# Four of 64 sets of expert weights loaded ahead of the experts stage instead of two, in one kernel on one core

## The reference, cut to what matters

```python
x = x + _L1_ffn_ref(_layernorm(x), gate_w, w_gate, w_up, w_down, sh_gate, sh_up, sh_down)
# in it: H = 512, F = 352, E = 64, TOP_K = 6, CAP = 128
scores = softmax(x @ gate_w.T)                 # 64 experts
topk_w, topk_idx = top_k(scores, 6)            # six experts a token
...                                            # each expert takes its first 128 tokens
g = silu(einsum('ech,ehf->ecf', buf, w_gate))
u = einsum('ech,ehf->ecf', buf, w_up)
d = einsum('ecf,efh->ech', g * u, w_down)      # weighted by topk_w, added per token
y = y + silu(x @ sh_gate.T) * (x @ sh_up.T) @ sh_down.T
```

## Time and profile before

| | us |
|---|---|
| median of three executions (lowest, highest) | 1879.22 (1876.37, 1886.87) |
| the profiled execution: its own time | 1880.75 |
| its span, first to last instruction | 1878.6 |
| TensorE busy | 1695.0 (90% of the span) |
| VectorE, ScalarE, POOL busy | 1099.2, 703.2, 618.2 |
| mean granted clock of TensorE | 0.962 |
| router phase, by the trace | about 1085 to 1331 |
| experts phase | 1331 to the end |

### The profile page before, as it was taken

The page is one execution under the profiler, slowest core; times in us unless marked ns, Lnnn a source line. Parts: engine busy times, 40 slices in busy tenths (PEclk is TensorE's granted clock), DMA queues, the critical chain, the costliest instruction groups (busy, mean ns, idle before and its releaser), DMA issues. The chain is left out here.

```text
span 1878.6 us, 22625 instructions
## 1 busy us (share of the span) xinstructions
PE 1695.0 (90%) x7201; PEld 1183.1 (63%) x7201; DVE 1099.2 (59%) x2381; ACT 703.2 (37%) x1330; POOL 618.2 (33%) x862
## 2 busy tenths in 40 slices
PE   6997999999998898989858999999799999999995
PEld 5885555555456676766646767676577666666664
DVE  5434766766644767776758567788544444444442
ACT  3120555555532454545432242212133333333332
POOL 2001433333640434343454141111224434334432
PEclk9997899999998999999978999999899999999998
DMA  7236356665423400000010021112699999999995
GB/s 252 102 123 193 91 152 166 177 168 152 116 61 105 165 1 0 1 1 1 1 57 31 1 69 48 46 38 105 217 348 331 329 324 335 337 320 329 329 321 126
DMA packets 120677, 284.81 MB, mean 152 GB/s; under 512 B 23472, under 2 KB 35248, under 8 KB 120304
## 3 DMA queue, kind: packets, MB, share of 16 engines
q1 hardware_dynamic: 106224, 247.71, 38.5%
q0 software_dynamic: 14336, 35.66, 9.0%
HBM read 224.03 MB, written 54.69 MB: 148 GB/s over the span
## 5 line engine op out<-in xcount | busy, mean ns | idle before, releaser
L1868 POOL DMA_INDIRECT out_x<-e_y,row_out x64 | 140.2, 2191 | 315.1 <-DVE row_out L1950 169.8
L831 ACT ACTIVATE probs<-bank 128x512 f32<-128x512 f32 (+3 forms) x384 | 167.6, 502 | 193.6 <-PE bank L779 192.2
L1098 PE MATMUL bank<-ln_xt_hi,gu_codes 128*128 128x512 f32 x352 | 154.1, 438 | 32.6 <-ACT gate_sum L1113 12.5
L754 PE MATMUL bank<-k_stack,q_stack 96*128 96x512 f32 (+3 forms) x384 | 147.6, 406 | 28.1 <-DMA k_stack<-qk_parts 16.7
L1903 PE MATMUL bank<-w_gate,xgt 128*128 128x352 f32 x512 | 163.5, 463 | 0.0
L1903 PE MATMUL bank<-w_up,xgt 128*128 128x352 f32 x512 | 161.9, 460 | 0.0
L874 DVE CUSTOM_DVE_ANT_0 masked_scores<-bank,wide_mask 128x128 bf16<-128x128 f32 (+3 forms) x256 | 116.2, 483 | 60.4 <-PE bank L754 59.4
L703 POOL TENSOR_SCALAR_AFFINE_SELECT probs<-probs 128x128 f32<-128x128 f32 x256 | 78.6, 322 | 204.5 <-ACT probs L831 200.5
L1099 PE MATMUL bank<-ln_xt_lo,gu_codes 128*128 128x512 f32 x352 | 144.6, 411 | 0.0
L793 PE MATMUL bank<-probs,v_ones 128*64 128x512 f32 (+3 forms) x768 | 143.9, 512 | 0.0
L779 PE MATMUL bank<-q_stack,k_stack 98*128 98x512 f32 (+3 forms) x384 | 140.9, 382 | 1.9 <-ACT probs L831 1.6
(11 more groups left out here) (255 smaller groups left out, 3867.1 us busy)
## 6 DMA issues: line engine op xcount, KB each, us to landing
w_gate<-in_w_gate SPq DMA_DIRECT2D x64, 704.0 KB, 6.9
w_up<-in_w_up SPq DMA_DIRECT2D x64, 704.0 KB, 9.0
w_down<-in_w_down SPq DMA_DIRECT2D x64, 512.0 KB, 9.1
q_stack<-qk_parts SPq DMA_DIRECT2D x96, 128.0 KB, 4.0
k_stack<-qk_parts SPq DMA_DIRECT2D x96, 128.0 KB, 4.2
w_down<-in_w_down SPq DMA_DIRECT2D x64, 192.0 KB, 9.9
qk_parts<-qk_stage_hi SPq DMA_DIRECT2D x32, 256.0 KB, 2.0
qk_parts<-qk_stage_lo SPq DMA_DIRECT2D x32, 256.0 KB, 2.3
```

Source lines behind the costliest of these rows:

```text
L754: pe.matmul(m.bank[MAXB[at % 3]][:, 0:cols], qs[slot][j][0:ROWS, q * P:(q + 1) * P], ks[slot][j][0:ROWS, half * CH:half * CH + cols], star ...
L831: act.activation(probs[u % PROBS][:, 0:cols], m.bank[EXPB[u % 3]][:, 0:cols], ACT.Exp, scale=scale).then_inc(exp_ready, 1)
L1098: pe.matmul(bank[:, :], gu[:, k, w], hi[:, k, :], start=True, stop=False)
L1868: pool.indirect_dma_start(out=a["out"][:, :], out_offset=bass.IndirectOffsetOnAxis(ap=row_out[e % YS][:, :], axis=0), in_=y[e % YS][:, :], ...
```

## The change

`PREFETCHED` goes from 2 to 4. Set 0 lies at `m.stage_at` (over the staged shared weights), sets 1 and 2 from `m.after_slots` on, set 3 at the top, over the normalized rows and their turned halves. Set 0 is loaded in chunk 0, after the store of the scores and a wait for `down_ready` of 2; sets 1 and 2 after the last up product; set 3 right after them and after a wait that the last normalized rows are stored. Sets 4 and 5 follow in the experts phase's memory, and the small buffers `row_in`, `row_out` and six of eight `xg` move behind sets 0 and 3. The experts phase's loop of loads then begins at expert 4.

```diff
-PREFETCHED = 2
+PREFETCHED = 4
+WEIGHT_SET = 4 * (2 * KT * F + (F // P + 1) * D)
...
+    gate_w_at = arena.at
...
-    m.experts = experts_weights(Arena(nc, m.after_slots), range(PREFETCHED))
+    m.rows_at = SBUF_END - 4 * (TPC * D + 2 * KT * CH)
+    m.experts = [experts_weights(Arena(nc, at), [e])[0] for e, at in
+                 enumerate((m.stage_at, m.after_slots, m.after_slots + WEIGHT_SET, m.rows_at))]
+    assert m.stage_at + WEIGHT_SET <= m.rows_at and m.after_slots + 2 * WEIGHT_SET <= gate_w_at
...
+            def prefetch(e):
+                load_gate_up(sp, a, m.experts[e], e, prefetched)
+                load_down(sp, a, m.experts[e], e, prefetched)
+
             for c in range(NCH):
...
                 sp.dma_start(score_rows[:, tiles, :], scores[:, :, 0:E]).then_inc(scores_stored, 16)
+                if c == 0:
+                    sp.wait_ge(down_ready, 2)
+                    prefetch(0)
                 if c + 1 == NCH:
                     sp.wait_ge(up_done, GS * NCH)
-                    for e in range(PREFETCHED):
-                        load_gate_up(sp, a, m.experts[e], e, prefetched)
-                        load_down(sp, a, m.experts[e], e, prefetched)
+                    prefetch(1)
+                    prefetch(2)
+                    sp.wait_ge(xn_stored, 16 * (NCH + 1))
+                    prefetch(3)
...
-    arena = Arena(nc, m.after_slots + PREFETCHED * 4 * (2 * KT * F + (DOWN_FULL + 1) * D))
+    arena = Arena(nc, m.after_slots + 2 * WEIGHT_SET)
+    stage_rest, rows_rest = Arena(nc, m.stage_at + WEIGHT_SET), Arena(nc, m.rows_at + WEIGHT_SET)
...
-    row_in = [arena.put(f"row_in{i}", [P, 1], U32) for i in range(AHEAD)]
-    row_out = [arena.put(f"row_out{i}", [P, 1], U32) for i in range(YS)]
-    xg = [arena.put(f"xg{i}", [P, XS], F32) for i in range(AHEAD)]
+    row_in = [stage_rest.put(f"row_in{i}", [P, 1], U32) for i in range(AHEAD)]
+    row_out = [rows_rest.put(f"row_out{i}", [P, 1], U32) for i in range(YS)]
+    xg = [(stage_rest if i < 3 else rows_rest if i < 6 else arena).put(f"xg{i}", [P, XS], F32) for i in range(AHEAD)]
```

More of the change, by code:

```diff
@@ L1820, in experts_phase @@
     y = [arena.put(f"e_y{i}", [P, D], F32) for i in range(YS)]
-    assert arena.at <= SBUF_END
+    assert arena.at <= m.stage_at and stage_rest.at <= m.rows_at and rows_rest.at <= SBUF_END
     XB, GATEB, UPB, HB, YB = 0, (1, 2), (3, 4), 5, (6, 7)
```

## The result

| | before | after |
|---|---|---|
| median of the executions, us | 1880.53 (4) | 1853.39 (4) |
| lowest, highest | 1876.37, 1886.87 | 1847.48, 1857.82 |
| the recorded execution's span | 1878.6 | 1853.9 |

The ratio is 0.9861, 95% interval 0.9833 to 0.9889: faster by 1.4%, 27 us. The sign was forecast, the size was not: 10 us were, and the result lies under the range.

What follows compares the result with a forecast made beforehand. DMA work was taken to pace the experts stage. Two sets' 11.3 us less a 1.5 us gap gave 9.8, the cross-check 10.2 to 11.5; 10 us was taken, about 1869.3 us against the median, range 1864.5 to 1877.

Steps and rivals of the forecast that it cites:

- Steps 1 and 2: Router: loading set 0 early and three sets after the last up product costs nil; without the cover, 2 and 6 us.
- a router that ends later than 1331: End of the router: it was to stay at 1331; a later end would show the third set is not covered.
- Step 3: Start of the experts stage: scatter 0 stays in place, its backlog, two sets now, is about nil by then.
- Step 4: Behind scatter 0: two sets' 11.3 us of queue time are saved, less an idle gap of 1.5 us (bounds 0 to 3.5).
- Step 5's term: Early scatters, cross-check: eight slow cycles vanish, 7.65 us, plus 0.64 a cycle until the queue fills; 10.2 to 11.5 us.
- from scatter 8 on 8.27 again: Steady scatter chain: expected to keep its old cycle of 8.27 us, each scatter 9 to 11 us earlier.
- 5.67 + 2.63 = 8.30 us: Middle of the experts stage: DMA time per expert, weight set plus scatter and gather, taken as what paces the cycle.
- rival D: Steady chain from scatter 8 on: a thinner queue makes the engines less efficient; 4.5 us slower, 1883.7; chance 0.08.
- The alternation of long and short cycles: Scatter chain, tail: cycles of 6.7 and 9.2 us alternate; a shift of their order is worth about 1.5 us either way.
- A: First scatters: latency, not work, sets a scatter's landing, so cycles go straight to 8.27; gain 7.65 us; chance 0.22.
- B: Experts stage: all moved bytes count, with no gap after scatter 0; gain 13.1 us, 1866.1 against the median; chance 0.10.
- C: Experts stage: the loads were hidden anyway, SP waiting for buffers, not bandwidth; gain 0 to 4 us; chance 0.10.

Runs made afterwards that it cites:

- lolast kernels: VectorE's e_down_lo moved behind its e_ht_lo, once in the kernel before (median 1863.02 us) and once in the changed kernel (1854.49 us).
- before_lolast: The kernel before with VectorE's e_down_lo moved behind its e_ht_lo; median 1863.02 us, ratio to before 0.9913.
- before_rowring: The kernel before with 16 row_out columns in place of four; median 1868.26 us, ratio to before 0.9956.
- after_again: The changed kernel itself, nothing altered, executed and recorded a second time; median 1853.86 us, ratio to before 0.9845.
- before_y6: The kernel before with six y buffers and six row_out columns in place of four; median 1860.70 us, ratio to before 0.9919.
- three_sets: The changed kernel with set 3 loaded at the start of the experts stage, not in the router; median 1861.06 us of two executions.

## Why the prediction was wrong, step by step

**Steps 1 and 2** (set 0 in the early router, three sets at its end: cost nil) held. Set 0 went out at 1117.48, 1.15 us behind the score store, the out stores followed. The prediction named a router that ends later than 1331 as a sign that the third set is not covered; it ended at 1339, but 5.1 us of that come from the phases ahead of it, and what the router itself took more is found in kernels without the change as well. Last issue of set 3 and first out store on SP's timeline of after:

```profile
1314.87 1.75 SPq L1439 DMA_DIRECT2D w_down<-in_w_down  x1
1321.35 14.14 SPq L1558 DMA_DIRECT2D out_x<-x_residual  x4
```

**Step 3** (scatter 0 stays in its place, backlog nil) held: 23.8 us after the first gather, 23.2 before. **Step 4**'s gap is there: from 1362 to 1366 the engines are at shares of 0.36 and 0.56, which is some 2.2 us lost, where 1.5 were taken.

**Step 5's term** came out at 11.5 us over the first eight scatters (11.0 in the second recording), and by the pair of lolast kernels at 12.7 us in the stage and 8.5 in the medians, where 10 were forecast and 13.1 was the bound. Mechanism and size were right.

**The step that failed is that the chain goes on "from scatter 8 on 8.27 again"**, which step 5 rests on, as its gain ends once the queue has filled up; and under it the reading in the first part that 5.67 + 2.63 = 8.30 us of DMA work set the cycle, "and the scatter chain only shows it". The term for the other 48 cycles was put at nil, and measured 22.1 us in one recording and 10.5 in the other. What set 8.27 was the scatter chain itself, with the collision in most of its links: with the same loads, gathers and scatters the cycle is 7.84 in before_lolast and 7.83 in before_rowring. A share of time with packets in flight gives back the cycle that it is read from, if it is near 1.00 throughout; it is no floor under it. The DMA queues of the kernel after, 1500 to 1800:

```profile
q1 hardware_dynamic: 25700, 83.02, 72.0%
q0 software_dynamic: 8615, 21.35, 31.4%
```

The same way of reckoning gives 216 us for 38 sets and 94 us for 38 scatters, 5.68 and 2.48, or 8.16 where the cycle is 7.81. Bytes over time were the number to distrust it by: 330 GB/s over these 300 us before, 349 after, and before showed 348 in its early cycles. The prediction used that row for rival D only, a loss from thin queues. Those early cycles had a deep queue as well as short scatters, so the row alone does not say which made the rate; before_lolast does, with 346 GB/s in the middle, without the deep queue.

What the page of before did show and the prediction passed over: a mean of 2191 ns for POOL's scatters beside single ones of 1.57 us. Rows 5 show the 2.42 themselves, for scatters 8, 10 and 56. The alternation of long and short cycles, written off as worth 1.5 us, was the mark of the tie between VectorE and the landings.

**Rivals.** A, B and C priced the same term (7.65, 13.1, 0 to 4); B came nearest to the time, which is luck, as its 13.1 us are all of that term and the rest of the 27 came from another. None had a second term. D had the place right, the steady chain, and the sign wrong. The phrase "the middle of the run is the same cyclic system" was the error all of them shared: TensorE at 7.63 and a chain at 7.8 differ by so little that a start 11 us better lasts for most or all of the 64 experts. So the regime in which before spent its last 49 experts is entered late (expert 46 in after_again) or not at all.

## What to carry to other kernels

A share of 1.00 on the DMA engines said here that something was in flight, not that capacity was used up (1.00 at 327 GB/s before, 1.03 at 346 for the same transfers in before_lolast); check GB/s against the best stretch of the same kernel, and look whether the mean of a descriptor-writing instruction hides two values. Where an engine and a chain of transfers run within a few per cent of each other behind a ring of buffers (7.63 and 7.8 us here), an edit at the start can decide which of two regimes the rest is in, so price the regimes, not only the edit. And where one event releases both VectorE and POOL, look at what each does in the next two microseconds: moving one VectorE operation behind another was worth 16 us of 1880 here without touching a DMA.

## What was not expected of the hardware

A scatter's time on POOL is 1.57 us alone and 2.42 us when VectorE's e_down_lo (two inputs and an output in the on-chip memory) has begun 0.25 us before it: 0.85 us, and 0.43 us in the cycle of before (8.27 against 7.84). When e_down_lo begins after the scatter, the two overlap at no cost to the scatter in 160 of 168 cases. With that collision out of the chain the same mix of loads, gathers and scatters moved at 346 to 351 GB/s in the middle of the stage (before_lolast) in place of 327 to 332. Twice a row of scatters landed some 1.5 us later than usual with the engines at 271 to 289 GB/s (before_y6 and three_sets); no trace here explains it.
